# Products for q moved from the first group of weight rows to the third and fourth, in turn with the dots for the maxima

## What is computed

```python
def _L2_attn_ref(embeddings, W_Q, W_K, W_V):
    Q = embeddings @ W_Q
    K = embeddings @ W_K
    V = embeddings @ W_V
    scores = jnp.einsum('bqd,bkd->bqk', Q, K) * scale        # scale = 1/sqrt(32)
    masked = jnp.where(causal[None, :, :], scores, -inf)     # causal: 3136 x 3136, lower triangle
    probs = jax.nn.softmax(masked, axis=-1)
    return jnp.einsum('bqk,bkd->bqd', probs, V)
...
t = t + _L2_attn_ref(_ln_t(t), L2_attn_W_Q, L2_attn_W_K, L2_attn_W_V)
```

## Time and profile before

| | us |
|---|---|
| median of 3 runs | 5225.98 (5218.76 to 5230.42) |
| the profiled execution | 5203.04 |
| its span, first to last instruction | 5201.3 |
| L2 attention, first Q to last work | from 1715 to about 3220 |
| L3 attention | from 3449 to about 4950 |

### The profile page before, as it was taken

One profiled execution on the slowest core, in us unless ns is written; L12 is line 12 of the kernel. 1 busy time (PEld: TensorE's weight loads), 2 busy tenths in 40 slices (PEclk: granted clock), 3 DMA queues, 4 the chain that ended last, 5 costly groups with the idle time before them and its releaser, 6 DMA issues. The chain is left out here.

```text
span 5201.3 us, 102304 instructions
## 1 busy us (share of the span) xinstructions
PE 4473.6 (86%) x39002; PEld 2775.7 (53%) x39002; DVE 3218.9 (62%) x6562; ACT 2836.1 (55%) x5790; POOL 1475.1 (28%) x2257
## 2 busy tenths in 40 slices
PE   4888888886754899999999997679999999999955
PEld 2666666665322455555555554555555555555544
DVE  4777777776796466666666564336666666666532
ACT  2766676665654356555555554315555555655521
POOL 3111111111354333334243322023333243333100
PEclk8998999988877799999999998769999999999966
DMA  1100000000000000000000000000000000000003
GB/s 26 27 2 2 2 2 2 2 2 3 1 1 0 1 2 2 2 2 2 2 2 2 2 2 5 1 1 2 2 2 2 2 2 2 2 2 2 2 5 49
DMA packets 348174, 22.44 MB, mean 4 GB/s; under 512 B 346388, under 2 KB 347700, under 8 KB 347700
## 3 DMA queue, kind: packets, MB, share of 16 engines
q1 hardware_dynamic: 347700, 16.03, 4.2%
HBM read 7.88 MB, written 6.42 MB: 3 GB/s over the span
## 5 line engine op out<-in xcount | busy, mean ns | idle before, releaser
L551 DVE TENSOR_REDUCE L2a_mx<-L2a_r 128x1 f32<-128x512 f32 (+4 forms) x1344 | 771.0, 627 | 334.2 <-PE L2a_r L415 326.8
L551 DVE TENSOR_REDUCE L3a_mx<-L3a_r 128x1 f32<-128x512 f32 (+4 forms) x1344 | 770.8, 627 | 331.3 <-PE L3a_r L415 323.7
L415 PE MATMUL L2a_r<-L2a_vT,L2a_qT 32*128 32x512 f32 (+3 forms) x3488 | 885.5, 529 | 13.2 <-DVE L2a_mx L551 12.5
L415 PE MATMUL L3a_r<-L3a_vT,L3a_qT 32*128 32x512 f32 (+3 forms) x3488 | 881.8, 527 | 12.9 <-DVE L3a_mx L551 12.3
L514 ACT ACTIVATE L2a_e<-L2a_r 128x512 f32<-128x512 f32 (+3 forms) x1344 | 669.1, 569 | 266.8 <-PE L2a_r L394 263.3
L514 ACT ACTIVATE L3a_e<-L3a_r 128x512 f32<-128x512 f32 (+3 forms) x1344 | 669.0, 569 | 266.7 <-PE L3a_r L394 263.2
L394 PE MATMUL L2a_r<-L2a_qT,L2a_vT 32*128 32x512 f32 (+4 forms) x3488 | 772.4, 513 | 2.8 <-DMA L2a_qT<-L2a_nm 2.7
L394 PE MATMUL L3a_r<-L3a_qT,L3a_vT 32*128 32x512 f32 (+4 forms) x3488 | 770.8, 511 | 3.8 <-DMA L3a_qT<-L3a_nm 3.8
L415 PEld LDWEIGHTS L2a_r<-L2a_vT,L2a_qT 32*128 32x128 f32 x3488 | 387.4, 190 | 158.5 <-DVE L2a_mx L551 90.1
L415 PEld LDWEIGHTS L3a_r<-L3a_vT,L3a_qT 32*128 32x128 f32 x3488 | 385.8, 189 | 156.7 <-DVE L3a_mx L551 89.8
L1471 POOL TENSOR_SCALAR win_xw<-win_xr,win_rs,win_sh 32x343 f32<-32x343 f32 (+7 forms) x432 | 186.5, 446 | 937.0 <-DVE win_sh L1340 936.9
(11 more groups left out here) (376 smaller groups left out, 7573.8 us busy)
## 6 DMA issues: line engine op xcount, KB each, us to landing
L2a_qT<-L2a_nm SPq DMA_DIRECT2D x768, 0.5 KB, 2.0
L3a_qT<-L3a_nm SPq DMA_DIRECT2D x768, 0.5 KB, 2.0
T<-in_x SPq DMA_DIRECT2D x16, 384.0 KB, 3.8
out<-T SPq DMA_DIRECT2D x16, 384.0 KB, 4.0
win_mq<-win_nmt SPq DMA_DIRECT2D x256, 3.1 KB, 1.7
win_msk<-in_L_conv_pos_emb SPq DMA_DIRECT2D x49, 0.2 KB
L2a_qT<-L2a_nm SPq DMA_DIRECT2D x32, 0.2 KB, 1.8
L3a_qT<-L3a_nm SPq DMA_DIRECT2D x32, 0.2 KB, 1.8
```

Source lines behind the costliest of these rows:

```text
L415: return nc.tensor.matmul(bank_of(x)[:, o:o + c1 - c0], QT_[g0:g0 + C, img % 2, q0:q0 + P], VT[g0:g0 + C, img % 2, c0:c1], start=start, st ...
L551: return nc.vector.tensor_reduce(to, frm, AX.X, ALU.max)
```

## The change

Q takes its rows in turn with the maxima: of the sequence of all maxima and Q in `WORK`, each takes group 2 or 3 by its place. `A` is made in partitions 64 to 127 in place of 0 to 31, for which the product that makes it is issued twice. A maximum after a Q may thereby use the other group than before.

```diff
+    GROUP = {x: C * (2 + n % 2) for n, x in enumerate(y for y in WORK if y[0] in ("max", "q"))}
...
-        A = sb("A", [C, QT, C])
+        A = sb("A", [P, QT, C])
...
-                nc.tensor.matmul(ACC[0:C, 0:C], WQB[:], WKB[:], start=True, stop=True).then_inc(w_mm, 1)
+                for g in (2, 3):
+                    last = nc.tensor.matmul(ACC[g * C:(g + 1) * C, 0:C], WQB[:], WKB[:], start=True, stop=True)
+                last.then_inc(w_mm, 1)
...
-                nc.vector.tensor_scalar(A[:], ACC[0:C, None, 0:C].to_broadcast([C, QT, C]), float(C) ** -0.5, None,
+                nc.vector.tensor_scalar(A[2 * C:], ACC[2 * C:, None, 0:C].to_broadcast([2 * C, QT, C]), float(C) ** -0.5, None,
                                         ALU.mult).then_inc(w_out, 1)
...
-                        g0 = C * (2 + n % 2)
+                        g0 = GROUP[x]
...
-                        nc.tensor.matmul(bank_of(x)[:, 0:w], A[:].rearrange("p r c -> p (r c)"),
-                                         VT[0:C, img % 2, f * QB:f * QB + w],
+                        g0 = GROUP[x]
+                        nc.tensor.matmul(bank_of(x)[:, 0:w], A[g0:g0 + C].rearrange("p r c -> p (r c)"),
+                                         VT[g0:g0 + C, img % 2, f * QB:f * QB + w],
                                          start=True, stop=True).then_inc(item_full, 1)
```

## The result

The changed kernel takes 5234.8 us (median of 14 runs, 5217.9 to 5243.5), the kernel before 5216.9 us on the same chips (14 runs, 5205.4 to 5230.4; the three runs shown ahead of the prediction all lay above that median). The ratio is 1.0033, interval 1.0022 to 1.0045: some 17 us slower. The measured time lies in the forecast range; the forecast of no change beyond 0.2% did not hold.

The account below looks back on a forecast made before the run. PE sets the pace (busy 197 of 200 us), through its in-order list, free row groups and bank hand-backs. -22.2 + 18.9 + 3 + 0.4 = +0.1 us leaves the median at 5226; range 5206 to 5248.

Parts of the forecast that it names:

- f = 1 and 2: Order `s s m m Q Q s s m m`, images' second and third Q: late even score freed earlier, 0.74 us a place, -22.2 us.
- f = 5: Order `s s m m Q mask`, Q after the DMA wait: Q queues behind a maximum, delaying mask; 0.63 us a place, +18.9 us.
- the even score is not late: Group 0 behind two queued Q: once emptied, the even score can start at about 2326.4; DVE can begin 0.8 us earlier.
- 0.77 - 0.14 = 0.63: Mask delay of 0.77 us before the edge maximum, less 0.14 of DVE's 0.17 us idle time: 0.63 us a place.
- The clock: Rival 3: small shifts decide which stretches run slow, 1.58 us each; seven more or fewer give 5215 or 5237; chance 0.17.
- The slow side of the clock: Slower half of the granted-clock rival: seven more long stretches, 11 us, 5237; half of chance 0.17, counted as 0.08.
- a new fall behind f = 5: After the Q following the DMA wait, where PE will work in one group alone: a clock fall, on the slow side.
- f = 0, 3, 4 and 6: The other places of Q in an image: nothing changes at each; -6 to +3 us kept for these together.
- the 0.2 us of f = 4: Q before the DMA wait: score gains 0.4 us, PV some 0.2, which goes into the wait: nothing.
- The start of the layers: Only maxima run, in groups 2 and 3, Q was free in group 0: +1.5 x 2 = +3 us (0 to +5).
- f = 0 and 1: First two Q at a layer's start, alone: in two groups the second overlaps, about 1 us saved.
- The setup: One more product of 32 columns a layer, two records: +0.2 x 2 = +0.4 us (0 to 1).

## Why the prediction was right and where it was wrong

The measured time lies in the range because the two main terms, a gain at f = 1 and 2 and a loss at f = 5, exist and have about the forecast sizes. That the 5234.8 us lie only 9 us from the forecast 5226 is partly luck: the median before has moved from 5226.0 to 5216.9 with more runs, and against that the change cost 17 us where +0.1 was forecast. The same range laid around 5216.9 would be 5197 to 5239 and would still hold it.

**f = 1 and 2: right.** 0.71 us a place against 0.74, -21.3 against -22.2 us, by the steps named: the second Q passes beside the first, the even score is not late, and DVE and ACT are released by 0.8 us earlier. One point of the picture is sharper now: either Q alone would have done.

**f = 5: the mechanism right, the price wrong by one subtraction.** Q begins 0.96 us behind the first maximum and mask comes 0.77 us later, as forecast. The step that failed is "0.77 - 0.14 = 0.63": I took 0.14 of the 0.17 us of DVE's idle time in front of the edge maximum for slack that would absorb part of the delay. The row itself names what ended that idle time: PE. An engine that sits idle until PE releases it has no slack against PE; a later PE is seen in full, and it was, 0.77 us. This makes 30 x 0.78 = 23.4 us in place of 18.9, 4.5 us.

**The clock: named as a rival, put at nothing in the sum.** The slow side of the clock, a new fall behind f = 5 with it, had half of 0.17. It took place, and with 13.7 us in the first trace it is the larger part of the miss. The rival priced seven stretches at 11 us, a little under what seven cost here. The long stretches between f = 0 and f = 1 went from 16 to 13 and gave 4.7 us back in these two traces; in others they range from 7 to 17, which is up to 14 us between single traces, so that they are no part of the change that can be told.

**The rest: right.** f = 0, 3, 4 and 6 cost and gain nothing that can be told; that the 0.2 us of f = 4 went into the wait for the DMAs agrees with the growth of that wait by 0.15 us a place, but other kernels without f = 4 moved have up to 0.11 of it. The start of the layers cost 1.0 us in the trace and 3 in the kernel of its own (0.9995 to 1.0018), against 3 forecast and neither told from nothing; at f = 0 and 1 the 1 us was saved (0.97). The setup took 0.03 us a layer in place of 0.2.

**The sum by what was measured.** -21.3 + 38.4 + 1.0 = +18.1 us in the traces, beside 17 us measured. As parts in kernels of their own: -20 + 28 + 3 = +11 us, or +4 with the second run of f = 5 alone (21); what is missing to 17 is within their intervals, and has the size of the falls that come with f = 1, 2 and 5 moved together.

**What stays open.** Why the falls need the pair. The idle time before the slot of f = 5 and the lone Q behind it are there with f = 5 moved alone as well, and it had one fall in each of two traces. What differs is the spacing of the images, shorter by 0.71 us. That the spacing decides was argued, not shown; and three falls came with the Q of f = 5 left in group 0. PE's idle time in front of the slot does not decide it alone either (rows in the last section).

## What to carry to other kernels

Ask of each item in an in-order queue what stands directly behind it: here an item was free in a group while the others had as much to do, and cost nearly its whole length (0.78 of 0.86 us) in front of work that needs all groups. Where one instruction of a rule gains and another loses, the rule should be split by place: the same change held a gain of 21 us and a loss of 38. And idle time of an engine is slack only against those that did not end it.

## What the runs showed of the hardware that was not expected

That results of matmuls in different groups are reported in the order of the list was read from one place before, and the ends of matmuls that it rests on are modelled by the profile; the runs agree with it: with either Q moved, so that the even score is no longer late, DVE's idle time there fell from 1.25 to 0.42 or 0.47 us.

The granted clock, which in the kernel before fell in 16 of 28 stretches behind f = 0 and in none behind f = 5, fell behind f = 5 in 6 to 9 of 30 after a change that moved 0.8 us of one group's work. How long PE sat idle in front of the slot does not tell which: image 6's slot came after 0.81 us of idle time and the clock fell to half (0.51), image 7's after 0.84 us and the clock stayed at 1.00, and image 9's, before which the trace shows no wait of PE, had a fall (2561.09 to 2573.10, mean 0.86).

```profile
2281.16 0.66 PE L399 MATMUL L2a_r<-L2a_qT,L2a_vT 32*128 32x512 f32 x1 [0.81 <-DMA L2a_qT<-L2a_nm]
...
2375.15 0.66 PE L399 MATMUL L2a_r<-L2a_qT,L2a_vT 32*128 32x512 f32 x1 [0.84 <-DMA L2a_qT<-L2a_nm]
```

```profile
2282.60:2289.40 6.80, 6.80 (x39) 0.51 0.01 0
...
2376.11:2386.92 10.81, 10.67 (x87) 1.00 0.06 0
```
